# Splitting the nine projection matmuls of a step in the first layer's schedule

## The reference

```python
# first sublayer (attention), 16 heads of 32
qkv = einsum('bse,oe->bso', layernorm(x), Wqkv_w) + Wqkv_b        # 512 -> 1536
q, k = rotary(qkv[:, :, 0]), rotary(qkv[:, :, 1]); v = qkv[:, :, 2]
attn = softmax(q @ (k / sqrt(32)).T + causal)
x = x + attn @ v
# second sublayer: quantised projections (fp8 values), self and cross attention, output projection
x = x + xattn(layernorm(x), ctx_2048)
# third sublayer: ternary weights, silu(gate) * up, rms norm, projection down
x = x + ffn(layernorm(x))
```

## Time and profile before

| | |
|---|---|
| median of three runs | 1234.28 us |
| the profiled execution's own time | 1234.7 us |
| its span, first to last instruction | 1232.9 us |
| PE busy | 1169.3 us (95%) |
| DVE busy | 920.0 us (75%) |
| ACT busy | 805.0 us (65%) |
| POOL busy | 618.1 us (50%) |
| L510, the 288 matmuls concerned | 76.2 us, first at 12.6 us, last at 165.1 us |

### The profile page before, as it was taken

How to read it: one execution, slowest core, us unless ns; L and a number is a source line. 1 busy time by engine, 2 the same in 40 slices (tenths; PEclk the granted TensorE clock), 3 DMA queues, 4 the chain that set the end, 5 groups by cost and what they waited for, 6 DMA issues and landing times.

```text
span 1232.9 us, 19189 instructions
## 1 busy us (share of the span) xinstructions
PE 1169.3 (95%) x6272; PEld 783.2 (64%) x6330; DVE 920.0 (75%) x2785; ACT 805.0 (65%) x2295; POOL 618.1 (50%) x769
## 2 busy tenths in 40 slices
PE   4989989889999999999999999999999999799998
PEld 2667767556666666676666766667676666555564
DVE  4569977999878877798999976657788777556242
ACT  4666548777878886676667765567876767663230
POOL 1637884654554554555566642215554455158072
PEclk9989898889999999999999999999999999899999
DMA  8210001212110231213232221022111110000000
GB/s 269 87 59 25 26 17 33 85 35 69 53 52 19 65 94 48 75 45 107 90 111 76 69 86 51 18 86 81 57 60 43 60 35 1 1 1 1 35 1 26
DMA packets 27475, 69.26 MB, mean 56 GB/s; under 512 B 2944, under 2 KB 9216, under 8 KB 27376
## 3 DMA queue, kind: packets, MB, share of 16 engines
q1 hardware_dynamic: 27104, 67.67, 17.4%
q10 hardware_dynamic: 272, 0.36, 0.1%
HBM read 61.21 MB, written 6.82 MB: 55 GB/s over the span
## 4 chain that ended last, share of the span: by engine, by line
PE 55%; DVE 20%; ACT 16%; POOL 5%; issue 2%; DMA 2%; ACTq 0%; POOLq 0%; SPq 0%
PE ps L870 11%; PE ps L1158 8%; PE ps L1089 6%; PE ps L860 5%; ACT big L799 5%; PE ps L1210 4%; PE ps L1037 4%; PE ps L967 3%; PE ps L510 3%; DVE big L415 3%; PE ps L1002 2%; PE ps L810 2%; DVE big L243 2%; ACT big L970 2%; DVE big L990 2%
## 5 line engine op out<-in xcount | busy, mean ns | idle before, releaser
L870 PE MATMUL ps<-big 128*125 128x512 bf16 x1152 | 264.6, 379 | 0.0
L799 ACT ACTIVATE big<-ps,big 112x128 f32<-112x128 f32 (+1 forms) x512 | 192.8, 457 | 73.9 <-POOL big L433 71.0
L870 PEld LDWEIGHTS ps<-big 128*125 128x125 bf16 x1152 | 155.2, 136 | 80.1 <-ACT big L961 0.3
L432 POOL TENSOR_TENSOR big<-big 112x4 f32<-112x4 f32 (+1 forms) x128 | 38.9, 304 | 308.4 <-ACT big L427 308.4
L860 PE MATMUL ps<-big 128*112 128x512 bf16 x768 | 189.3, 390 | 4.5 <-ACT big L961 2.0
L666 POOL TENSOR_TENSOR big<-big 128x448 f32<-128x448 bf16 x96 | 102.9, 1072 | 104.1 <-DVE big L984 63.1
L860 PEld LDWEIGHTS ps<-big 128*112 128x112 bf16 x768 | 100.6, 133 | 69.6 <-issue 8.0
L970 ACT ACTIVATE big<-ps,big 112x375 f32<-112x375 f32 x128 | 74.8, 584 | 84.5 <-DVE big L969 83.4
L415 DVE BATCH_NORM_STATS2 big<-ps 112x6 f32<-112x128 f32 (+1 forms) x512 | 113.4, 284 | 20.1 <-PE ps L870 16.5
L1037 PE MATMUL ps<-big 125*128 125x224 f32 (+1 forms) x512 | 120.9, 359 | 6.8 <-DVE big L1019 5.6
L990 DVE TENSOR_SCALAR big<-big 112x112 f32<-112x112 f32 (+1 forms) x256 | 117.7, 481 | 6.8
(11 more groups left out here) (115 smaller groups left out, 2279.2 us busy)
## 6 DMA issues: line engine op xcount, KB each, us to landing
big<-in_ctx_t SPq DMA_DIRECT2D x32, 375.0 KB, 3.5
big<-in_w_s SPq DMA_DIRECT2D x16, 512.0 KB, 4.1
big<-in_w_p SPq DMA_DIRECT2D x16, 512.0 KB, 4.5
big<-in_w_x SPq DMA_DIRECT2D x16, 512.0 KB, 3.7
big<-in_w_g SPq DMA_DIRECT2D x16, 512.0 KB, 3.7
big<-in_w_d SPq DMA_DIRECT2D x8, 512.0 KB, 4.6
big<-in_w_a SPq DMA_DIRECT2D x8, 384.0 KB, 5.1
scr<-big SPq DMA_DIRECT2D x24, 128.0 KB, 1.7
```

What stands on the lines that cost most here:

```text
L799: t = act(lambda e, j=j: e.activation(z[0:rows, 128 * j:128 * j + 128], bk[0:rows, 128 * j:128 * j + 128], ACT.Identity, bias=rr[0:rows, 4 ...
L870: t = pe(lambda e, k=k, s=s, u=u, n=n: e.matmul(bk[0:CK, :], cT[:, s, k, CK * c:CK * c + CK], w[:, u, k, col:col + 512], start=n == 0, sto ...
```

## The change

`a_mm` gets a second argument: half 0 issues the first five of the nine matmuls of a part, half 1 the other four. In every tick half 0 now comes behind `a_s2` and `a_tq`, ahead of `a_s0`, and half 1 behind `a_s3`, ahead of `l_2` and `a_tr`. The lags of the parts (3, 4, 5, 6) stay, and so do number, operands and waits of the matmuls; the lists of the other engines keep their order. The bank of q is now taken behind `a_s2` of tick 3 and no longer at that tick's end.

```diff
-        def a_mm(it, part):
+        def a_mm(it, part, half):
             xT = it["xT"]
-            for m in range(9 * part, 9 * part + 9):
+            for m in range(9 * part + 5 * half, 9 * part + 5 + 4 * half):
...
-            if part == 3:
+            if (part, half) == (3, 1):
                 a_xT.release(it["xTi"], t)
                 marks["a_mm"] = t
...
                 (8, lambda it: a_tq(it, 0)),
                 (9, lambda it: a_tq(it, 1)),
-                (6, lambda it: a_mm(it, 3)),
+                *((3 + p, lambda it, p=p: a_mm(it, p, 0)) for p in range(4)),
                 ("h", 2, a_s2e),
...
-                (5, lambda it: a_mm(it, 2)),
-                (4, lambda it: a_mm(it, 1)),
                 ("h", 3, a_s3),
+                *((3 + p, lambda it, p=p: a_mm(it, p, 1)) for p in range(4)),
                 (lead + 9, l_2),
...
                 (1, a_tr),
-                (3, lambda it: a_mm(it, 0)),
                 (0, a_h),
```

## The result

The changed kernel took 1242.9 us (median of 4 runs, 1240.08 to 1243.46), the kernel before in the same comparison 1233.47 us (4 runs). The ratio is 1.0069, 95% interval 1.0057 to 1.0081: 8.5 us slower by the ratio (the two medians are 9.4 us apart). The profiled execution took 1242.82 us with a span of 1241.0, against 1234.7 and 1232.9, so the trace shows 8.1 us of it. The forecast was 1236.4, and its range ended at 1241.5, under the measured time.

The account below looks back on a forecast made before the run. VectorE and GpSimd, blocking each other, were taken to set the round of 20.39 us, not TensorE. The terms 0 + 0.9 + 2.2 - 0.9 + 0 gave +2.2 us, forecast 1236.4 us, range 1231.5 to 1241.5.

Parts of the forecast that it names:

- (a): Part 0's clock dips on TensorE go with the even spread; counted at 0 us, bounds 0 and -2.1.
- (b): New TensorE wait on L498 at the head of tick 3, later scores; 0.3 us a round, +0.9 us, bounds 0 and 2.7.
- the ring: VectorE and GpSimd hold each other through L665, L666, L668 and rotary operations, setting the pace; TensorE isn't in it.
- R2: New idle time at tick 3's wait on L498 lowers the clock each round; about 1242 us, chance 0.20.
- (c): Tick 19, weight-load pause: scores behind half 0 delay L702 and L340; +2.2 us, shift between 0.5 and 3.9.
- (d): Start, L581 at 40.65: scores stand behind five matmuls instead of nine; -0.9 us, bounds -0.9 and 0.
- (e): Evictions and banks of q, k and v: 0 us, unknown bank waits at most about 1 us.
- R1: TensorE sets the pace, part 0's clock dips go and 6.0 us are gained; 1228.3 us, chance 0.12.
- R3: Wait and cover cancel, shifts at tick 19 and the start too; no change, 1234.3 us, chance 0.18.

Follow-up runs that it names:

- The version with part 0 at the end: Changed kernel with part 0 whole at the end of tick 3, parts 1 to 3 still split; 1233.6 us, ratio 0.9996 to the kernel before.

## Why the prediction was wrong

The direction and the mechanism were right: the wait on L498 is at the head of the ticks that I named, and VectorE's L581, ScalarE's L702 and VectorE's L340 are late at tick 19. The size was a quarter of the measured one: +2.2 us in the sum where 8.5 came. By the steps:

(a) The dips at 0. Right. The version with part 0 at the end has a clock of 1.00, TensorE idle, and a round of 20.37 us. The kernel with the new order up to sequence 4 has the same with the old order. The chain of waits, which named TensorE from 84 to 160 us (one of its steps is in rows 2), couldn't show that: it follows idle time, and VectorE has none while it stands blocked by GpSimd; that is inside the listed duration of L663 and L665.

(b) The step that failed. I took 0.3 us for each of three rounds, because I read the long L663 at 130.38 as slack that would cover a late L581. The lateness itself was about right: L581 of tick 3 waits 0.53 us where the sum had 0.5, and L581 of tick 1 comes 13.18 us behind L498 (109.38 to 122.56) where it had 13.1, against 12.14 before (13.1 less 12.14 is 1.0, not the 0.9 that I wrote). What failed is the cover: the round at full clock became 1.09 us longer, so nothing of this was covered, and 0.63 of it is the wait on L498. What fills the "slack" is on GpSimd. The operations of tick 23, GpSimd of the kernel after and VectorE of the same tick:

```profile
112.64 1.99 POOL L668 TENSOR_TENSOR big<-big 128x448 bf16<-128x448 f32 x1
114.60 1.30 POOL L536 TENSOR_TENSOR big<-big 112x512 f32<-112x512 f32 x1
```
```profile
109.38 0.61 DVE L498 TENSOR_TENSOR big<-ps,big 128x448 bf16<-128x448 f32 x1
...
112.59 0.62 DVE L581 TENSOR_REDUCE big<-ps 112x4 f32<-112x448 f32 x1 [0.53 <-PE ps L575]
113.13 0.61 DVE L662 TENSOR_TENSOR big<-big 128x448 bf16<-128x448 f32 x1
113.78 0.99 DVE L663 TENSOR_SCALAR big<-big 128x448 bf16<-128x448 bf16 x1
...
122.56 0.62 DVE L581 TENSOR_REDUCE big<-ps 112x4 f32<-112x448 f32 x1 [0.34 <-PE ps L575]
```

and L668 in the kernel before, one round on:

```profile
129.87 1.37 POOL L668 TENSOR_TENSOR big<-big 128x448 bf16<-128x448 f32 x1
```

GpSimd's L668 starts 3.26 us after L498 in both kernels (109.38 to 112.64, 126.61 to 129.87). It is listed with 1.37 us before and 1.99 after, 0.62 longer, and the L536 behind it starts 1.33 us after it before (at 131.20) and 1.96 after. That is near what L581 was late by (0.53) and to the round's 0.63. L668 ends 0.9 us behind the end of VectorE's L662 in both, so it looks as if L662 holds it up, and a late L662 passes its delay to GpSimd, whose list is in the ring. The changed kernel has the counterpart too, one round on, where L581 is so late that L662 comes only when L668 is over:

```profile
134.10 1.03 POOL L668 TENSOR_TENSOR big<-big 128x448 bf16<-128x448 f32 x1
```
```profile
134.92 0.62 DVE L581 TENSOR_REDUCE big<-ps 112x4 f32<-112x448 f32 x1 [1.41 <-PE ps L575]
135.47 0.61 DVE L662 TENSOR_TENSOR big<-big 128x448 bf16<-128x448 f32 x1
```

Without L662 beside it, L668 takes 1.03 us. L663 keeps its 0.99 us because all around it has moved too. The Trainium skill (SBUF — State Buffer, "Who interferes with whom") has this: a VectorE operation with both inputs in SBUF contends with GpSimd's reads. I had cited that section and used the half of it that speaks of two-port modes; L662 here has two SBUF inputs. By the rows the loss is shown; that the port is its cause is argued from them and the section, not tested by itself. One point doesn't fit: as my prediction put the rule, the second of the two waits until the first is done, but L668 is listed as starting 0.49 us before L662 (112.64 and 113.13), and it is L668 that is longer while L662 keeps its 0.61 us. Starts on GpSimd are rough in the profile, so this stays open.

The second part of (b), the clock after the idle time, stood in the sum at nothing; I had it as R2, with 0.20 and a place in every round. It came in one of three, behind 2.12 us of idle time, and that round cost 2.79 us against 1.09. With it (b) is 4.3 us against the 0.9 of the sum.

(c) Tick 19: +2.2 predicted, 0.5 to 3.9 as bounds. L340 came at 95.17 against 92.59, with a start 1.05 us earlier, so 3.63 us; TensorE stayed at half clock through the product with v and `l_2`, as in the upper bound. Another 0.57 us come before tick 22, where L581 of tick 21 waits 1.50 us for its scores. Here most of a wait was covered, as I had assumed for (b): in the kernel before, L646 and L663 of that tick are listed with 1.74 and 1.23 us, after it with 0.83 and 0.28. So cover exists in some places and has to be read for each. I had taken the middle where the low clock before and behind the pause spoke for the upper end.

(d) The start: -0.9 predicted, -1.05 in the trace. That isn't a confirmation, since a kernel with the old order there shows -0.86 and one with the new order -0.24.

(e) No bank wait of note shows: 0, as said. In sum: 4.3 + 4.2 - 1.05 and the 0.6 us behind tick 34 are the 8.1 us of the trace.

R1 (faster) and R3 (no change) fall. R2 was nearest in time (about 1242) with its mechanism in part: half clock behind one of three waits and not behind each.

## What to carry to other kernels

When work is moved towards the head of an in-order list, look first at what its first instruction waits for and how far that producer lags, and then at everything behind it: here 5 matmuls, 1.1 us of work put ahead of the scores, cost 8.5 us in sum. An engine that looks full may be blocked inside its instructions; compare the duration of one form where the other engine is idle and where it isn't (0.28 and 0.99 us here) before believing that the chain's engine sets the pace, and don't count a blocked operation as slack without asking which engine the delay would reach next. Idle time put in front of large matmuls has a second price, the clock, which comes in some rounds and not in others: it needs a chance and a price of its own in the sum.

## What the runs showed of the hardware

The same order of small and large matmuls had TensorE drop to half clock in the kernel before (nine matmuls listed with 3.10 and 4.05 us instead of 2.11) and not in the kernel with the new order up to sequence 4 only, whose nine at the same places, from tick 23 on, are listed with 2.11 or 2.15 us. In the version without rotary embedding the clock is 1.00 from 90 to 140 us, and nine matmuls at 145.55 are listed with 3.31 us. So the order alone doesn't tell where the clock falls.

The idle time ahead of part 0 doesn't alone tell it either. In the kernels whose part 0 stands at the head of tick 3, idle times of 2.12, 2.13 and 2.36 us from tick 23 on were each followed by matmuls at half clock; none of 1.15, 1.13, 0.93, 0.64 and 0.63 us was. In between there was both. Of two of 1.75 us, in the kernel with part 0 alone moved, one left the five matmuls behind it at 1.26 us and one brought 1.68 us. In the same kernel 1.34 us, ahead of 41.58, brought 2.15 us, and 1.47 us in the changed kernel without rotary embedding, ahead of 57.70, left 1.26. The wait of 1.86 us near 60 us left them at 1.26 us in the changed kernel (60.59) and brought 2.35 us in the one with the new order up to sequence 4 (60.32).
